# Transformer block in split fp16: output products of the last batch moved between the last score units and behind the last AV

## The chip, the cores and the metric

The kernel runs on one core of one Trainium2 chip. The metric is the device time of one execution, in microseconds (us). Three executions before the change took 1926.81, 1930.75 and 1939.71 us; the median is 1930.75 us.

## The reference

For x of 16 batches x 512 rows x 512 values, with xn the layer norm of x over its last axis, the reference computes

```
x + attention(xn) + ffn(xn)
attention: q, k, v = xn @ w_qkv.T + b_qkv; 16 heads of 32; softmax(causal(q k.T / sqrt(32))) v; then @ w_out.T + b_out
ffn:       (silu((xn @ gate.T) * gate_s) * ((xn @ up.T) * up_s)) @ down.T * down_s      (512 -> 1408 -> 512)
```

## The kernel before

**Number format.** Every fp32 operand is split into a high and a low fp16 half, and a product is the sum of three fp16 products (high x high, high x low, low x high). The gate, up and down weights are ternary, so for them two products do.

**Groups and units.** A batch has four groups of four heads, so there are 64 groups (0 to 63, `NGRP`). The scores of a group are worked off in ten units, `U = 10`, numbered n = 0 to 639 (`NU` = 640). I call those of the last group unit 0 to unit 9 (n = 630 to 639). A unit is one PSUM bank of score tiles (widths 512, or 384 + 128, or 256 + 256); four banks (0 to 3) are used in turn. Each unit passes through these steps:

- TensorE: `scores(n)`, 1 or 2 products (tile `stk`), which wait until the low half of unit n - 4 is done (`v_lo`), since the bank is used again.
- VectorE: `maximum(n)` (line 548; it appears as ISA or CUSTOM_DVE_ANT_0). ScalarE: `exponent(n)` (L466).
- VectorE: `reciprocals` once for two units (L539), ScalarE scales them (L454).
- ScalarE: `high(n)` (L458) writes the high half of the probabilities to `phl`; VectorE: `low(n)` (L558) the low half.
- SyncE: `turn_p` (L912) turns the finished tiles with a DMA transpose into `pt`. The queue issues them in program order. The last three transposes of a group wait for the low halves of unit 8 (two of them) and of unit 9 (the last one).
- TensorE: `av(G)`, 48 products of 32 columns of weights (tiles `pt`, `vv`), two score units into the next group; of the last group it stands at n = 644 (`NU + AV_K`). ScalarE drains it (L434), POOL splits it into `att` (L752 high, L754 low, semaphore `p_al`).

**The rest of a batch's end.** `down_product(b, t)` makes 128 rows (t = 0 to 3) of the down projection: 22 products of 512 columns. VectorE scales the result (`down_scale`, L592, into the buffer `q_0`) and POOL adds it to `res` (`down_add`, L781). The output projection of 128 rows is 12 products of 512 columns (`out_products`), three for each of the four groups of the batch. In the last batch nine of them per row block, those of the first three groups, are issued ahead of the last AV (36 in all), into banks 4, 5, 0 and 1 (`early_bank`), and the three of the last group behind it (12 in all). VectorE adds the result to `res` (`out_add`, L585), and SyncE stores it (L958).

**The flag.** The fast path holds only for inputs in range. VectorE gathers the tests in `check_end` (L613 to L628, 12 instructions), TensorE sums the flags over the partitions with one fp32 product (line 391), VectorE turns it into an integer in `check_flag` (L632 to L637). Behind the block all engines meet at a barrier (L963), load the flag (L52), and branch over the general path (L55).

**What sets the order.** All five engines run a program written out by hand in a loop over n; within a step n the calls stand in a fixed order. TensorE issues in program order, and so do the others: an instruction that waits holds up all behind it. `d_at`, `av_at` and, for the change, `early_at` say at which n a product stands.

Of the kernel before, what the change touches and what calls it, by code (L numbers as in the profile page):

```python
# [46 lines left out]
def fused_block(nc, x, w_qkv, b_qkv, w_out, b_out, gate, up, down, gate_s, up_s, down_s, out):  # L47
    B = x.shape[0]
    args = (B, x, w_qkv, b_qkv, w_out, b_out, gate, up, down, gate_s, up_s, down_s, out)
    with ExitStack() as ctx:  # L50
        flag = fast_path(nc, ctx, *args)
        general = nc.values_load(flag[0:1, 0:1], min_val=0, max_val=3)  # L52
    with nc.If(general > 0), ExitStack() as ctx:
        general_path(nc, ctx, *args)
    nc.end_ifs()  # L55
# [11 lines left out]
def fast_path(nc, ctx, B, x, w_qkv, b_qkv, w_out, b_out, gate, up, down, gate_s, up_s, down_s, out):  # L67
# [3 lines left out]
    NU = U * NGRP  # L71
    NF = 2 * NI * B
# [16 lines left out]
    bq, gsh, cis, half, ones = (carve(n) for n in (12, NI, NI, 1, 1))  # L89
# [4 lines left out]
    flag, flag_i = fl[0:1, 0:4], fl[0:1, 4:5].bitcast(I32)  # L94
    flag_p = lst[0]
# [36 lines left out]
    d_last = sem("d_last")  # L132
    d_y = [sem(f"d_y{i}") for i in range(4)]
# [15 lines left out]
    for b in range(B):  # L149
        if b == 0:  # L150
            v_at[0] = (0, 1, 0)
            v_at[1] = (0, 1, 1)
        else:
            v_at[40 * b] = (b, 0, 0)
            v_at[40 * b + 1] = (b, 0, 1)
            v_at[40 * b + 17] = (b, 1, 0)
            v_at[40 * b + 29] = (b, 1, 1)
        for t, k in enumerate((19, 21, 37, 39)):
            d_at[40 * b + k] = (b, t)
        if b < B - 1:  # L160
            for t, k in enumerate((47, 48, 49, 51)):
                o_at[40 * b + k] = (b, t)
# [27 lines left out]
            res_at[16 + t if b == 0 else 40 * b + (12, 13, 15, 17)[t]] = (b, t)  # L190
    LAST = NU + 6
    early_bank = [bank[i] for i in (4, 5, 0, 1)]

# [54 lines left out]
    def tensor_program(eng):  # L250
# [42 lines left out]
        def av(G):  # L293
            b, g = divmod(G, 4)
            for qt in range(3):
                w.wait_ge(d_pt[qt][0], 16 * (2 * G + 2))
            for p in range(2):
                w.wait_ge(d_pt[3][p], 16 * (G + 1))
            w.wait_ge(v_vl, 4 * b + 2 * (g // 2) + 2)
            bk = job_bank_free(("av", G))  # L300
            for kt in range(4):
                for k, (vp, pp) in enumerate(((0, 0), (1, 0), (0, 1))):
                    for j in range(4):
                        step = 12 + 2 * (j % 2) + pp
                        a = step * kt + 2 * (j % 2) + pp + kt
                        i = mm(bk[32 * j:32 * j + 32, 128 * kt:512], vv[:, vp, kt, 128 * g + 32 * j:128 * g + 32 * j + 32],
                               pt[j // 2][:, a:a + step * (3 - kt) + 1:step, :], kt == 0 and k == 0, kt == 3 and k == 2,
                               tile_position=(0, 32 * j))
            i.then_inc(s_av, 1)

        def out_products(bk, t, lo, hi):
            prods = [(kt, ap, wp) for kt in range(4) for ap, wp in ((0, 0), (0, 1), (1, 0))]
            for kt, ap, wp in prods[lo:hi]:
                i = mm(bk[:, :], att[:, ap, kt, 128 * t:128 * t + 128], wout[:, wp, kt], kt == 0 and not ap and not wp, kt == 3 and ap == 1)
            return i

        def o(b, t):
            for k in range(4):
                w.wait_ge(*ready["wout", k])
            w.wait_ge(p_al, 4 * b + 4)  # L320
            bk = job_bank_free(("o", b, t))
            out_products(bk, t, 0, 12).then_inc(s_o, 1)
# [39 lines left out]
        for n in range(LAST):  # L362
            if n < NU:
                scores(n)
            if NU <= n < NU + 4:
                t = n - NU
                w.wait_ge(p_al, 4 * B - 1)
                w.wait_ge(v_fh, NF // 2)
                w.wait_ge(v_fa, NF)
                if t >= 2:  # L370
                    w.wait_ge(v_lo, NU - 5 + t)
                out_products(early_bank[t], t, 0, 9).then_inc(s_oe, 1)
            if n in d_at:
                down_product(*d_at[n])
            if n in av_at:
                av(av_at[n])
            if n in qk_at:
                qk(*qk_at[n])
            if n in v_at:
                v(*v_at[n])  # L380
            if n in o_at:
                o(*o_at[n])
            for f in f_at.get(n, ()):
                gate_up(f)
        w.wait_ge(s_oe, 4)
        w.wait_ge(p_al, 4 * B)
        for t in range(4):
            out_products(early_bank[t], t, 9, 12).then_inc(s_o, 1)
        w.wait_ge(v_chk, 1)
        w.wait_ge(v_lo, NU)  # L390
        eng.matmul(bank[3][0:1, 0:3], ones[:, :], flag_p[:, 0:3], start=True, stop=True).then_inc(s_flag, 1)


    def scalar_program(eng):
# [114 lines left out]
    def vector_program(eng):  # L509
# [166 lines left out]
        for n in range(LAST):  # L676
            if n % 2 == 0 and 2 <= n <= NU:
                reciprocals(n - 2)
            if n < NU:
                maximum(n)  # L680
            if n - 1 in d_at:
                down_scale(*d_at[n - 1])
            for f in f_at.get(n - 1, ()):
                hidden(f)
            if 2 <= n <= NU + 1:
                low(n - 2)
            if n - 1 in v_at:
                v_low(*v_at[n - 1])
            if n - 1 in o_at:
                out_add(*o_at[n - 1])  # L690
            if n in norm_at:
                b, t = norm_at[n]
                w.wait_ge(d_xin[t % 2], 16 * xin_turn["norm", b, t])
                statistics(4 * b + t, t, xin[t % 2][:, :])
            if n - 4 in norm_at:
                b, t = norm_at[n - 4]
                hl = xhl[t % 2]
                w.wait_ge(p_xh, 4 * b + t - 3)
                w.wait_ge(v_xs, 4 * b + t + 1)
                eng.tensor_tensor(hl[:, 1], xin[t % 2][:, :], hl[:, 0], ALU.subtract).then_inc(v_xl, 1)  # L700
            if n - 2 in norm_at:
                b, t = norm_at[n - 2]
                scaled(4 * b + t, t, xin[t % 2][:, :])
            if n - 1 in wout_at:
                wout_low(wout_at[n - 1])
            if n in peak_at:
                check_peak(peak_at[n])
            if 0 <= n - 40 * (B - 1) < 19:
                check_most(n - 40 * (B - 1))
            if n == NU:  # L710
                check_end()
        for t in range(4):
            out_add(B - 1, t)
        check_flag()


    def gpsimd_program(eng):
# [165 lines left out]
    def sync_program(eng):  # L883
# [72 lines left out]
        for t in range(4):  # L956
            w.wait_ge(v_oy, 4 * (B - 1) + t + 1)
            eng.dma_start(out[B - 1, 128 * t:128 * t + 128, :], res[t][:, :]).then_inc(d_last, 16)  # L958
        for t in range(4):
            w.wait_ge(d_y[t], 16 * (B - 1))  # L960
        w.wait_ge(d_last, 64)

    with nc.Block() as block:  # L963
        block.tensor(tensor_program)
# [2 lines left out]
        block.gpsimd(gpsimd_program)  # L967
        block.sync(sync_program)

    return flag_i  # L970


def general_path(nc, ctx, B, x, w_qkv, b_qkv, w_out, b_out, gate, up, down, gate_s, up_s, down_s, out):
# [217 lines left out]
```

## Time and profile before

| | |
|---|---|
| median of three executions | 1930.75 us |
| the profiled execution, its own time | 1925.77 us |
| its span | 1922.4 us |
| granted TensorE clock, mean | 0.996 of full |
| PE busy | 1858.9 us (97%) |
| DVE busy | 1505.5 us (78%) |
| ACT busy | 1443.0 us (75%) |
| POOL busy | 1264.4 us (66%) |

The span is the time from the first to the last recorded instruction; the execution's own time is 3.4 us longer. PE is TensorE, DVE is VectorE, ACT is ScalarE, POOL is GpSimd, SPq is the queue of SyncE. A name such as L252 is the line of the kernel; all large products are issued from one helper, so they have the same line and are told apart by their tiles.

### The profile page before, as it was taken

To read this page: it belongs to the slowest core of one execution; us is meant where nothing else is said; L and a number is where in the kernel's file an instruction comes from. 1 tells how busy PE (TensorE), PEld (TensorE's weight loads), DVE (VectorE), ACT (ScalarE), POOL (GpSimd) and SP (SyncE) were. 2 spreads that over 40 slices of the span, in tenths; PEclk is the share of its full clock that TensorE was granted. 3 is DMA by queue.
4 is the path that set the end of the run, shared out by engine and by line. 5 is a ranking of instruction groups with operands and counts; after the bars stand their busy time and mean duration, and the time that the engine had idled before them with its cause. 6 is when DMAs were issued, how large, how long until landed. Compare 5 with 4: busy or idle time off the path is not lost.

```text
span 1922.4 us, 44220 instructions
## 1 busy us (share of the span) xinstructions
PE 1858.9 (97%) x14978; PEld 1220.4 (63%) x14978; DVE 1505.5 (78%) x4516; ACT 1443.0 (75%) x4263; POOL 1264.4 (66%) x1799
## 2 busy tenths in 40 slices
PE   6889999999999999999999999999999999999996
PEld 4556666666656666676666666666566666766663
DVE  4887778787787877778777787877878777787885
ACT  4786777868778787787867778687787877778684
POOL 5765857758576685766758576575666757576462
PEclk9999999999999999999999999999999999999998
DMA  9978969879797897979889798886978779687684
GB/s 227 160 158 159 186 130 194 149 159 181 132 197 144 171 168 136 196 132 190 152 155 187 133 192 134 161 159 134 189 128 169 150 140 183 131 182 138 121 163 94
DMA packets 818551, 305.93 MB, mean 159 GB/s; under 512 B 756176, under 2 KB 793168, under 8 KB 818320
## 3 DMA queue, kind: packets, MB, share of 16 engines
q1 hardware_dynamic: 796176, 240.79, 69.6%
q0 software_dynamic: 22144, 62.27, 13.0%
q8 instruction: 119, 1.95, 0.4%
q14 instruction: 112, 0.92, 0.1%
HBM read 55.59 MB, written 16.78 MB: 38 GB/s over the span
## 4 chain that ended last, share of the span: by engine, by line
PE 75%; DVE 11%; POOL 5%; ACT 5%; issue 2%; DMA 2%; SPq 1%; POOLq 0%; ACTq 0%; DVEq 0%
PE bank L252 75%; DVE phl L558 3%; ACT phl L458 2%; DVE bank L548 2%; DVE res L585 1%; ACT bank L466 1%; DVE xhl L700 1%; POOL ht L771 1%; DVE small L523 1%; DMA pt<-phl 1%; POOL qkp L744 1%; DVE fh L573 1%; DVE ft L568 1%; POOL att L754 0%; POOL ht L769 0%
## 5 line engine op out<-in xcount | busy, mean ns | idle before, releaser
L466 ACT ACTIVATE bank<-bank,small 128x512 f32<-128x512 f32 (+3 forms) x1024 | 516.8, 506 | 215.2 <-DVE small L548 214.6
L558 DVE SCALAR_TENSOR_TENSOR phl<-bank,small,phl 128x512 f16<-128x512 f32 (+3 forms) x1024 | 526.1, 545 | 139.3 <-ACT phl L458 136.2
L548 DVE CUSTOM_DVE_ANT_0 bank<-bank,mask 128x512 f32<-128x512 f32 (+3 forms) x1024 | 483.6, 503 | 179.9 <-PE bank L252 177.4
L458 ACT ACTIVATE phl<-bank,small 128x512 f16<-128x512 f32 (+3 forms) x1024 | 501.0, 532 | 29.6 <-DMA pt<-phl 19.0
L252 PE MATMUL bank<-xnT,wg 128*128 128x256 f16 x2816 | 365.7, 272 | 4.5 <-DVE fh L573 4.5
L252 PE MATMUL bank<-xnT,wu 128*128 128x256 f16 x2816 | 364.9, 273 | 0.0
L252 PE MATMUL bank<-xnT,wqkv 128*128 128x512 f16 x1536 | 353.4, 380 | 2.8 <-DMA xnT<-xhl 2.8
L252 PE MATMUL bank<-wd,ht 128*128 128x512 f16 x1408 | 314.5, 379 | 4.4 <-POOL ht L771 4.4
L252 PEld LDWEIGHTS bank<-xnT,wg 128*128 128x128 f16 x2816 | 263.0, 97 | 65.5 <-DVE fh L573 5.3
L252 PEld LDWEIGHTS bank<-xnT,wu 128*128 128x128 f16 x2816 | 275.6, 98 | 31.9
L252 PE MATMUL bank<-stk 96*128 96x512 f16 (+3 forms) x1024 | 244.8, 300 | 16.0 <-DVE phl L558 11.9
L771 POOL TENSOR_TENSOR ht<-fh,ht 128x256 f16<-128x256 f32 x352 | 237.4, 675 | 29.3
L252 PEld LDWEIGHTS bank<-xnT,wqkv 128*128 128x128 f16 x1536 | 148.1, 98 | 169.5 <-issue 4.7
L765 POOL TENSOR_TENSOR fh<-fh,ft 128x256 f32<-128x256 f32 x176 | 127.9, 727 | 185.1 <-DVE ft L568 184.8
L252 PEld LDWEIGHTS bank<-wd,ht 128*128 128x128 f16 x1408 | 136.0, 98 | 161.9 <-POOL ht L771 6.7
L769 POOL TENSOR_SCALAR ht<-fh 128x256 f16<-128x256 f32 x352 | 144.1, 410 | 126.3 <-DVE fh L573 109.5
L415 ACT ACTIVATE ft<-bank,small 128x256 f32<-128x256 f32 x352 | 170.4, 485 | 71.9 <-PE bank L252 71.4
L466 ACT ACTIVATION_READ_ACCUMULATOR bank<-bank,small 128x1 f32 x1024 | 215.7, 211 | 0.0
L252 PE MATMUL bank<-wqkv,xnT 128*128 128x256 f16 x1536 | 181.3, 275 | 14.4 <-DMA xnT<-xhl 14.4
L252 PE MATMUL bank<-wout,att 128*128 128x512 f16 x768 | 178.6, 383 | 3.5 <-POOL att L754 2.9
L252 PEld LDWEIGHTS bank<-wqkv,xnT 128*128 128x128 f16 x1536 | 150.9, 99 | 39.6 <-DVE wqkv L515 14.4
L781 POOL TENSOR_TENSOR res<-res,q 128x512 f32<-128x512 f32 x64 | 81.2, 1268 | 144.2 <-DVE q L592 143.8
(97 smaller groups left out, 2193.1 us busy)
## 6 DMA issues: line engine op xcount, KB each, us to landing
stk<-qkp SPq DMA_DIRECT2D x768, 64.0 KB, 2.2
res<-in_x_dram POOLq DMA_DIRECT2D x64, 256.0 KB, 4.7
xin<-in_x_dram POOLq DMA_DIRECT2D x60, 256.0 KB, 3.9
out_dram<-res POOLq DMA_DIRECT2D x60, 256.0 KB, 4.2
pt<-phl SPq DMA_TRANSPOSE x512, 4.3
xin<-in_gate_dram POOLq DMA_DIRECT2D x11, 256.0 KB, 3.9
xin<-in_up_dram POOLq DMA_DIRECT2D x11, 256.0 KB, 4.6
xin<-in_down_dram POOLq DMA_DIRECT2D x11, 256.0 KB, 3.6
```

What stands on the lines that cost most here:

```text
L252: mm = lambda o, lhs, rhs, start, stop, **k: eng.matmul(o, lhs, rhs, start=start, stop=stop, skip_group_check=True, **k)
L415: eng.activation(ft[f % 3][:, :], bank[4 + f % 2][:, 0:256], ACT.Tanh, scale=gsh[:, k:k + 1]).then_inc(a_ft, 1)
L458: i = eng.activation(part(qt, j)[:, j % 2, 0], pb[:, off:off + W], ACT.Copy, scale=st_r[:, c:c + 1])
L466: i = eng.activation(pb[:, off:off + W], pb[:, off:off + W], ACT.Exp, bias=st_m[:, c:c + 1], scale=-1.0, accum_out=st_s[:, c:c + 1])
L523: eng.bn_stats(st[:, 0:6], xi).then_inc(v_bn, 1)
L548: i = eng.tensor_tensor_reduce(out=bk[:, off:off + W], in0=bk[:, off:off + W], in1=mask[:, 512 - W:512], scale=-(32.0 ** -0.5) / (QS * QS) ...
L558: i = eng.scalar_tensor_tensor(part(qt, j)[:, j % 2, 1], pb[:, off:off + W], st_r[:, c:c + 1], part(qt, j)[:, j % 2, 0], ALU.mult, ALU.sub ...
L568: eng.scalar_tensor_tensor(tt[:, :], tt[:, :], 1.0, bk[:, 0:256], ALU.add, ALU.mult).then_inc(v_fa, 1)
L765: eng.tensor_tensor(hh[:, :], hh[:, :], ft[f % 3][:, :], ALU.mult).then_inc(p_fm, 1)
L769: eng.tensor_scalar(hs[:, 0], hh[:, :], 1.0, 1.0, op0=ALU.mult, op1=ALU.mult).then_inc(p_hh, 1)
L771: eng.tensor_tensor(hs[:, 1], hh[:, :], hs[:, 0], ALU.subtract).then_inc(p_fl, 1)
L781: eng.tensor_tensor(res[t][:, :], res[t][:, :], dtmp[:, :], ALU.add).then_inc(p_dy, 1)
```

## The change

Six things change, all in the last batch or behind it:

1. The output products of row blocks 0 and 1 for the first three groups (18) move from behind the last score unit to between the units: six behind unit 6, nine behind unit 7, three behind unit 8 (`early_at`). They wait for POOL's split of groups 61 and 62 (`p_al`) and for the last hidden tiles (`v_fh`, `v_fa`).
2. The down products of row blocks 2 and 3 (44 products) move from n = 637 and 639 to n = 640 and 641, so both stand behind unit 9.
3. The output products of row blocks 2 and 3 for the first three groups (18) move behind the last AV (`early_behind_av`).
4. VectorE's `check_end` moves from n = 640 to n = 642, behind the low half of unit 9, and the flag product moves ahead of the last 12 output products.
5. `check_flag` stands ahead of the four last `out_add` instead of behind them.
6. SyncE's waits for the stores leave the block and stand behind the load of the flag, in front of SyncE's branch.

```diff
--- before.py
+++ after.py
@@ -48,8 +48,9 @@
     B = x.shape[0]
     args = (B, x, w_qkv, b_qkv, w_out, b_out, gate, up, down, gate_s, up_s, down_s, out)
     with ExitStack() as ctx:
-        flag = fast_path(nc, ctx, *args)
+        flag, stored = fast_path(nc, ctx, *args)
         general = nc.values_load(flag[0:1, 0:1], min_val=0, max_val=3)
+        stored()
     with nc.If(general > 0), ExitStack() as ctx:
         general_path(nc, ctx, *args)
     nc.end_ifs()
@@ -155,7 +156,7 @@
             v_at[40 * b + 1] = (b, 0, 1)
             v_at[40 * b + 17] = (b, 1, 0)
             v_at[40 * b + 29] = (b, 1, 1)
-        for t, k in enumerate((19, 21, 37, 39)):
+        for t, k in enumerate((19, 21, 37, 39) if b < B - 1 else (19, 21, 40, 41)):
             d_at[40 * b + k] = (b, t)
         if b < B - 1:
             for t, k in enumerate((47, 48, 49, 51)):
@@ -190,6 +191,9 @@
             res_at[16 + t if b == 0 else 40 * b + (12, 13, 15, 17)[t]] = (b, t)
     LAST = NU + 6
     early_bank = [bank[i] for i in (4, 5, 0, 1)]
+
+    early_at = {NU - 4: ((0, 0, 6),), NU - 3: ((0, 6, 9), (1, 0, 6)), NU - 2: ((1, 6, 9),)}
+    early_behind_av = {NU + AV_K: (2, 3)}
 
 
 
@@ -314,6 +318,19 @@
                 i = mm(bk[:, :], att[:, ap, kt, 128 * t:128 * t + 128], wout[:, wp, kt], kt == 0 and not ap and not wp, kt == 3 and ap == 1)
             return i
 
+        def early_products(t, lo, hi):
+            w.wait_ge(p_al, 4 * B - 2)
+            if hi > 6:
+                w.wait_ge(p_al, 4 * B - 1)
+            if t < 2:
+                w.wait_ge(v_fh, NF // 2)
+                w.wait_ge(v_fa, NF)
+            else:
+                w.wait_ge(v_lo, NU - 5 + t)
+            i = out_products(early_bank[t], t, lo, hi)
+            if hi == 9:
+                i.then_inc(s_oe, 1)
+
         def o(b, t):
             for k in range(4):
                 w.wait_ge(*ready["wout", k])
@@ -362,18 +379,14 @@
         for n in range(LAST):
             if n < NU:
                 scores(n)
-            if NU <= n < NU + 4:
-                t = n - NU
-                w.wait_ge(p_al, 4 * B - 1)
-                w.wait_ge(v_fh, NF // 2)
-                w.wait_ge(v_fa, NF)
-                if t >= 2:
-                    w.wait_ge(v_lo, NU - 5 + t)
-                out_products(early_bank[t], t, 0, 9).then_inc(s_oe, 1)
+            for t, lo, hi in early_at.get(n, ()):
+                early_products(t, lo, hi)
             if n in d_at:
                 down_product(*d_at[n])
             if n in av_at:
                 av(av_at[n])
+            for t in early_behind_av.get(n, ()):
+                early_products(t, 0, 9)
             if n in qk_at:
                 qk(*qk_at[n])
             if n in v_at:
@@ -382,13 +395,13 @@
                 o(*o_at[n])
             for f in f_at.get(n, ()):
                 gate_up(f)
-        w.wait_ge(s_oe, 4)
-        w.wait_ge(p_al, 4 * B)
-        for t in range(4):
-            out_products(early_bank[t], t, 9, 12).then_inc(s_o, 1)
         w.wait_ge(v_chk, 1)
         w.wait_ge(v_lo, NU)
         eng.matmul(bank[3][0:1, 0:3], ones[:, :], flag_p[:, 0:3], start=True, stop=True).then_inc(s_flag, 1)
+        w.wait_ge(s_oe, 4)
+        w.wait_ge(p_al, 4 * B)
+        for t in range(4):
+            out_products(early_bank[t], t, 9, 12).then_inc(s_o, 1)
 
 
     def scalar_program(eng):
@@ -707,11 +720,11 @@
                 check_peak(peak_at[n])
             if 0 <= n - 40 * (B - 1) < 19:
                 check_most(n - 40 * (B - 1))
-            if n == NU:
+            if n == NU + 2:
                 check_end()
+        check_flag()
         for t in range(4):
             out_add(B - 1, t)
-        check_flag()
 
 
     def gpsimd_program(eng):
@@ -956,9 +969,6 @@
         for t in range(4):
             w.wait_ge(v_oy, 4 * (B - 1) + t + 1)
             eng.dma_start(out[B - 1, 128 * t:128 * t + 128, :], res[t][:, :]).then_inc(d_last, 16)
-        for t in range(4):
-            w.wait_ge(d_y[t], 16 * (B - 1))
-        w.wait_ge(d_last, 64)
 
     with nc.Block() as block:
         block.tensor(tensor_program)
@@ -967,7 +977,12 @@
         block.gpsimd(gpsimd_program)
         block.sync(sync_program)
 
-    return flag_i
+    def stored():
+        for t in range(4):
+            nc.sync.wait_ge(d_y[t], 16 * (B - 1))
+        nc.sync.wait_ge(d_last, 64)
+
+    return flag_i, stored
 
 
 def general_path(nc, ctx, B, x, w_qkv, b_qkv, w_out, b_out, gate, up, down, gate_s, up_s, down_s, out):
```

TensorE, from unit 5 of the last group up to the last AV; the tiles say which product it is (`stk` scores, `wd` down, `wout` output). Before:

```order
L252 MATMUL bank<-stk 128x512 x2
L252 MATMUL bank<-stk 128x384
L252 MATMUL bank<-stk 128x128
L252 MATMUL bank<-wd,ht 128x512 x22
L252 MATMUL bank<-stk 128x384
L252 MATMUL bank<-stk 128x128
L252 MATMUL bank<-stk 128x256 x2
L252 MATMUL bank<-wd,ht 128x512 x22
L252 MATMUL bank<-wout,att 128x512 x36
L252 MATMUL bank<-pt,vv 32x512 x12
```

With the change, the same place of TensorE:

```order
L256 MATMUL bank<-stk 128x512 x2
L256 MATMUL bank<-wout,att 128x512 x6
L256 MATMUL bank<-stk 128x384
L256 MATMUL bank<-stk 128x128
L256 MATMUL bank<-wout,att 128x512 x9
L256 MATMUL bank<-stk 128x384
L256 MATMUL bank<-stk 128x128
L256 MATMUL bank<-wout,att 128x512 x3
L256 MATMUL bank<-stk 128x256 x2
L256 MATMUL bank<-wd,ht 128x512 x44
L256 MATMUL bank<-pt,vv 32x512 x12
```

Nothing is added: 44 down products and 18 of the 36 output products stand ahead of the AV, in another order, and 22 fewer products of 512 columns stand between units 7 and 8, nine in their place.

TensorE behind the last AV, from its last 12 products on. Before:

```order
L252 MATMUL bank<-pt,vv 32x256 x12
L252 MATMUL bank<-pt,vv 32x128 x12
L252 MATMUL bank<-wout,att 128x512 x12
L391 MATMUL bank<-small 1x3
L963 UNCONDITIONAL_BRANCH
```

With the change, the same place of TensorE:

```order
L256 MATMUL bank<-pt,vv 32x256 x12
L256 MATMUL bank<-pt,vv 32x128 x12
L256 MATMUL bank<-wout,att 128x512 x18
L400 MATMUL bank<-small 1x3
L256 MATMUL bank<-wout,att 128x512 x12
```

Eighteen output products and the flag product now stand between the AV and the last 12 products.

VectorE, from behind the row maximum of unit 8 (`low` of unit 7 is the 128x384 and 128x128 pair ahead of the reciprocal, `low` of unit 8 the pair behind it). Before:

```order
L592 TENSOR_TENSOR q_0<-bank,dsc 128x512
L558 SCALAR_TENSOR_TENSOR phl_1<-bank,small,phl_1 128x512
L548 ISA bank,small<-bank,mask 128x256
L548 ISA small 128x1
L548 ISA bank,small<-bank,mask 128x256
L548 ISA small 128x1
L558 SCALAR_TENSOR_TENSOR phl<-bank,small,phl 128x384
L558 SCALAR_TENSOR_TENSOR phl<-bank,small,phl 128x128
L539 RECIPROCAL small<-small 128x4
L592 TENSOR_TENSOR q_0<-bank,dsc 128x512
L558 SCALAR_TENSOR_TENSOR phl<-bank,small,phl 128x384
L558 SCALAR_TENSOR_TENSOR phl<-bank,small,phl 128x128
```

With the change, the same place of VectorE:

```order
L571 SCALAR_TENSOR_TENSOR phl_1<-bank,small,phl_1 128x512
L561 ISA bank,small<-bank,mask 128x256
L561 ISA small 128x1
L561 ISA bank,small<-bank,mask 128x256
L561 ISA small 128x1
L571 SCALAR_TENSOR_TENSOR phl<-bank,small,phl 128x384
L571 SCALAR_TENSOR_TENSOR phl<-bank,small,phl 128x128
L552 RECIPROCAL small<-small 128x4
L571 SCALAR_TENSOR_TENSOR phl<-bank,small,phl 128x384
L571 SCALAR_TENSOR_TENSOR phl<-bank,small,phl 128x128
L605 TENSOR_TENSOR q_0<-bank,dsc 128x512
L571 SCALAR_TENSOR_TENSOR phl<-bank,small,phl 128x256 x2
```

The two `down_scale` instructions have left their places ahead of the low halves of units 6 and 8; the first now stands ahead of the low half of unit 9, the second behind it.

## Rows read from the trace of the kernel before

**Rows 1.** The chain of waits, end of the span; columns: start us, length us, what.

```profile
1904.60 1.84 PE bank L252 x48
...
1909.31 5.29 PE bank L252 x12
...
1914.70 0.69 DVE res L585
```

**Rows 2.** Timeline of TensorE (PE), from 1880 us; start us, us, instruction, count, idle before.

```profile
1886.25 0.39 PE L252 MATMUL bank<-stk 96*128 96x384 f16 x2 [1.83 <-DVE phl L558]
1886.48 4.91 PE L252 MATMUL bank<-wd,ht 128*128 128x512 f16 x22
1891.23 0.60 PE L252 MATMUL bank<-stk 96*128 96x384 f16 x4
...
1896.42 7.93 PE L252 MATMUL bank<-wout,att 128*128 128x512 f16 x36
...
1914.52 0.19 PE L391 MATMUL bank<-small 128*1 128x3 f32 x2
```

**Rows 3.** Timeline of VectorE (DVE), from 1886 us.

```profile
1890.22 0.18 DVE L539 RECIPROCAL small<-small 128x4 f32<-128x4 f32 x1 [0.48 <-ACT bank L466]
1891.65 0.57 DVE L548 CUSTOM_DVE_ANT_0 bank<-bank,mask 128x384 f32<-128x384 f32 x1 [1.25 <-PE bank L252]
...
1892.38 0.69 DVE L592 TENSOR_TENSOR q<-bank,dsc 128x512 f32<-128x512 f32 x1
...
1897.30 0.87 DVE L558 SCALAR_TENSOR_TENSOR phl<-bank,small,phl 128x384 f16<-128x384 f32 x2
...
1899.69 0.87 DVE L558 SCALAR_TENSOR_TENSOR phl<-bank,small,phl 128x256 f16<-128x256 f32 x2
```

**Rows 4.** Timeline of ScalarE (ACT), from 1886 us.

```profile
1896.04 1.57 ACT L458 ACTIVATE phl<-bank,small 128x384 f16<-128x384 f32 x4
```

**Rows 5.** Timeline of GpSimd (POOL), from 1886 us.

```profile
1885.59 1.16 POOL L754 TENSOR_TENSOR att<-q,att 128x512 f16<-128x512 f32 x1
```

**Rows 6.** The last attention transpose, read by its tile; issue time, then DMA to landing.

```profile
L912 SPq DMA_TRANSPOSE pt<-phl x1: 1307/1307/1307, 1901.3 to 1901.3; - x1
...
DMA to landing us min/median/max: 3.2/3.2/3.2
```

**Rows 7.** Timeline of SyncE's queue (SPq) from 1898 us: the first of the last three transposes.

```profile
1898.19 1.41 SPq L912 DMA_TRANSPOSE pt<-phl  x1
```

**Rows 8.** Timeline of PE: idle times near three us, early in the span.

```profile
63.40 1.05 PE L252 MATMUL bank<-xnT,wg 128*128 128x256 f16 x8 [2.87 <-DVE fh L573]
...
87.73 0.39 PE L252 MATMUL bank<-stk 96*128 96x384 f16 x2 [2.79 <-DVE phl L558]
...
107.02 4.04 PE L252 MATMUL bank<-xnT,wqkv 128*128 128x512 f16 x12 [2.79 <-DMA xnT<-xhl]
```

**Rows 9.** Stretches of PE: start:end us, length, busy (count), granted clock, DMA share, GB/s.

```profile
62.50:63.40 0.90, 0.01 (x1) 1.00 0.52 77
87.00:87.70 0.70, 0.00 (x0) 1.00 1.17 214
106.00:106.50 0.50, 0.00 (x0) 0.75 1.30 280
109.50:110.00 0.50, 0.50 (x3) 0.83 1.15 211
1908.50:1909.00 0.50, 0.00 (x0) 0.50 0.00 0
1915.00:1915.50 0.50, 0.00 (x0) 0.68 1.02 385
```

**Rows 10.** SyncE's waits after 1900 us, by line; durations ns, first and last start.

```profile
L43 SPq EVENT_SEMAPHORE  x2: 28/28/28, 1915.8 to 1917.5; - x2
```

**Rows 11.** The branch behind the flag, by line: PE's own.

```profile
L55 PEldq COMPARE_BRANCH  x1: 3783/3783/3783, 1918.6 to 1918.6; - x1
```

**Rows 12.** DMA queues from 1918.6 us to the end: packets, MB, share.

```profile
q14 instruction: 4, 0.03, 2.9%
```

More of the change, by code:

```diff
@@ L384, in tensor_program @@
                 gate_up(f)
+        w.wait_ge(v_chk, 1)
+        w.wait_ge(v_lo, NU)
+        eng.matmul(bank[3][0:1, 0:3], ones[:, :], flag_p[:, 0:3], start=True, stop=True).then_inc(s_flag, 1)
         w.wait_ge(s_oe, 4)
@@ L388, in tensor_program @@
             out_products(early_bank[t], t, 9, 12).then_inc(s_o, 1)
-        w.wait_ge(v_chk, 1)
-        w.wait_ge(v_lo, NU)
-        eng.matmul(bank[3][0:1, 0:3], ones[:, :], flag_p[:, 0:3], start=True, stop=True).then_inc(s_flag, 1)
     def scalar_program(eng):
```

## The prediction

> **What bounds the kernel now.** I read the page first: PE is busy for 97% of the span, but the change touches only the last 40 us, so shares of the whole say nothing of it. The views that count are the chain of waits at the end, the timelines of PE, VectorE and SyncE's queue from 1880 us on, and the rows behind the last store.
>
> The chain ends in three stages. The last AV starts at 1904.60; from its end, 1906.4, to 1909.31 PE stands while ScalarE drains and POOL splits it; then twelve output products take 5.29 us and the last add starts at 1914.70 [rows 1]. The reader should see two things in it. First, the twelve products cost 5.29 / 12 = 0.44 us each, while the 36 ahead of the AV cost 7.93 / 36 = 0.22 us each [rows 1, 2]: the granted clock is 0.50, the 1.2 GHz level, from 1908.5 on, after PE had been idle for 2 us, and is back only at about 1915.3 [rows 9]. Second, the AV looks as if it were held by PE (the output products end at about 1904.4), but the last transpose is issued at 1901.32 and lands 3.2 us later, at 1904.5 [rows 6]. So both end together, and taking products away ahead of the AV does not bring it forward by itself: the transposes must come earlier too.
>
> Behind the last add SyncE waits for the stores from 1915.8 to 1917.5 [rows 10]; then come the barrier, the load of the flag, and PE's branch of 3.78 us from 1918.6, which is the end of the span [rows 11].
>
> **The transposes: what the new order moves.** The chain to them runs over units 8 and 9. Before, unit 8's scores stood behind 22 down products (1886.48 to 1891.23), and VectorE waited 1.25 us for them before its maximum at 1891.65 [rows 2, 3].
>
> - Now nine output products stand there. They wait for POOL's split, which ends at 1885.59 + 1.16 = 1886.75 [rows 5]; with 9 x 0.22 = 1.98 us PE comes to unit 8 at about 1888.9. VectorE has the reciprocal at 1890.22 ahead of it, about 0.1 us long to the next start, so the maximum starts at about 1890.3: 1.3 us earlier. PE has one us of slack here, should POOL be late.
> - The down scale of 0.61 us (0.69 in its row, overlapped with the next) leaves the place between the maximum of unit 8 and the low half of unit 6 [rows 3]. From there VectorE is 1.3 + 0.6 = 1.95 us ahead.
> - ScalarE gains between 1.3 (unit 8) and 1.95 (unit 9); I take 1.6, since unit 7's high half stands between the two exponents. Its last four high halves then start at 1896.04 - 1.6 = 1894.4, and the two of unit 8 are done half of 1.57 us later [rows 4], at 1895.25. VectorE used to be in the second down scale then and started the low half of unit 8 at 1897.30 [rows 3]. Now it starts at 1895.3: 2.0 us earlier.
> - The low half of unit 9 is now behind a down scale that waits for the first 22 down products. They start behind unit 9, at about 1890.0, and end at 1890.0 + 22 x 0.22 = 1894.9, before VectorE gets there. If that cover were gone, it would be late by what the products are late.
> - SyncE issued the three last transposes in a row from 1898.19 to 1901.32 [rows 6, 7], so it is the low half of unit 8 that sets them. I move the landing by 2.0: 1902.5, the AV to 1902.6. Bounds: 1.3 (only the maximum's gain survives) and 2.5.
>
> PE is done with its 44 down products at 1890.0 + 9.7 = 1899.7. So it now idles for about 2.75 us **ahead of** the AV, where it was busy before.
>
> **From the AV to the last twelve products.** AV 1.84 us, then 18 output products, 3.97 us, then the flag product. The split of the AV takes 1909.31 - 1906.4 = 2.9 us and is covered by the 3.97. [...] AV start to first of the twelve: 1.84 + 3.97 + 0.5 = 6.3 us against 4.7 before: **+1.6**.
>
> **The last twelve.** With no idle time ahead of them they run at the full clock, 12 x 0.22 = 2.64 us in place of 5.29: **-2.65**. The adds (0.61 us each) keep pace with three products (0.66 us). `check_flag` costs nothing: it runs on VectorE before the first of the twelve is drained. `check_end`, 12 small instructions, runs after the second down scale at 1900, and has until 1908. The last `down_add` (1.3 us on POOL) ends near 1902, before the AV is drained.
>
> **The stores.** SyncE no longer waits ahead of the barrier: **-1.75** (1915.8 to 1917.5 and its wake-up). The last store, 2 us in flight, then ends about 3 us before PE's branch does, so the moved wait is covered.
>
> **The sum:** -2.0 + 1.6 - 2.65 - 1.75 = **-4.8 us** against the profiled execution's own 1925.77 us, so 1921.0. That execution is 5 us below the median shown, which moved in the same way gives 1926. Of the four executions known, two stand within 1.1 us of each other near 1926, and two above; I forecast **1924 us**, between the two readings.
>
> The Trainium skill ("TensorE: Matmul & The Clock Gate", Part 1) says that the default state of the array's clock is throttled and that activity releases it. By that the 30 products behind the AV run at the full clock and the sum stays -4.8, provided the AV's work counts as activity; the rows at 1909 to 1915 show a stretch of products in which it had not yet been released, by which the twelve would give nothing and the sum would be -2.1.
>
> **The rivals.**
>
> *The clock falls in the new idle time (0.35).* Early in this trace PE idled for 2.87 and 2.79 us and kept the full clock, and once for 2.79 us and lost it about 2 us into the idle time; it came back after 3.3 us or so [rows 8, 9]. The idle behind the last AV, 2.9 us, lost it for 6.7 us [rows 1, 9]. My 2.75 us is in the middle of these, so this is nearly as likely as the forecast. Of 3.3 to 6.7 us at half clock about 0.7 are idle; the other 2.7 to 6.0 us do half the work, a loss of 1.3 to 3.0 us. Sum -3.5 to -1.8: 1922.3 to 1924.0 by the profiled execution's count, 1927 to 1929 by the median's.
>
> *The same fall, and the clock stays low to the end (0.03): the one that ends slower.* Place: AV, 18 and 12 products. Price: each of them twice as long, 1.84 + 3.97 + 0 (the twelve were slow before too). Sum -2.0 + 1.6 + 5.8 - 1.75 = +3.7, 1929.4. It decides once more than 9.5 us of work is at half clock (half of it eats 4.8). For it: before, twelve products in a row, 5.3 us, did not bring the clock back until they were over. Against it: nowhere in the trace does low clock last beyond 6.7 us.
>
> *The transposes don't move (0.07).* They were held by the low half, but the transpose of units 6 and 7's tiles is now issued 2 us nearer to the ones before it, and transposes wait for one another. Then AV at 1904.6, PE idle for 4.7 us, and clock surely lost for 3 us or more: 0 + 1.6 - 2.65 - 1.75 + 2 = -0.8, 1925.0.
>
> *The branch gets slower (0.05).* PE's 3.78 us go with instruction packets, four in one queue [rows 11, 12]. Should a store still be in flight hold them up, at most the 1.75 us come back: -3.0, 1922.8. The Trainium skill ("Runtime: NRT & Kernel Launch", Instruction fetch mechanics) says that a taken branch outside the loaded part of the program must fetch its target by DMA; the packets agree. By my times the last store lands at 1914.5 and the fetch begins about then, so they hardly meet.
>
> *The 18 products between units delay the chain instead of filling it:* the first six fit into PE's 1.83 us of idle time ahead of unit 7 [rows 2] (6 x 0.22 = 1.3 us), the nine are counted above, and the three (0.66 us) end before unit 9's bank is free. I give this no chance of its own.
>
> **How the numbers follow.** Forecast 0.50, clock lost for a while 0.35, clock low to the end 0.03, transposes unmoved 0.07, branch 0.05. The cases lie between 1921 and 1929.4 by the profiled execution, and 5 us higher by the median; the shown executions themselves spread over 13 us. I take the range from 1918 (the sum by the profile with the transposes at their upper bound and the flag at its lower, 1920.2, and some scatter) to 1932 (the second case by the median, and scatter). A measurement of this kernel can tell about 1% (19 us) from no change; no case comes near it in either direction, and the few hundredths left are for scatter. Faster by over 1%: 0.01; within 1%: 0.98; slower by over 1%: 0.01.
>
> **What the profile after would show.** Right: VectorE's maximum of unit 8 no longer waits for PE; the last transpose issued near 1899.3; the AV near 1902.6; no idle time on PE from the AV to the end of the twelve products; these at 0.22 us each; no wait for the stores ahead of the barrier; span about 1917.6. The clock row between 1900 and 1910 decides between the first two cases. Wrong: an AV still at 1904.5, a row for the low half of unit 9 that waits for a down scale, or a branch on PE that starts 4.8 us earlier and ends at the same time as before.

## The result, and the profile after

The change took **1922.34 us** in the median of 20 executions (1919.03 to 1935.46), the kernel before 1929.69 us in as many (1921.13 to 1940.35). The ratio of the two is 0.997, 95% interval 0.9958 to 0.9983: 3.3 to 8.1 us less, well under 1%. The profiled execution of the change has a span of 1918.6 us and an own time of 1921.82 us; before it was 1922.4 and 1925.77.

Two executions of one kernel are not alike before the end begins. Unit 6's scores start at 1884.03 in the profile of before (the row ahead of those of [rows 2]), at 1885.24 in that of the change, and between 1880.8 and 1896.1 over all the traces read below. So I compare the **tail**: from the start of unit 6's score product (the last one of 512 columns) to the end of the span. The row of before is

```profile
1884.03 0.39 PE L252 MATMUL bank<-stk 96*128 96x512 f16 x1 [1.17 <-DVE phl L558]
```

and the tail is 1922.4 - 1884.03 = 38.4 us before and 1918.6 - 1885.24 = 33.4 us with the change, 5.0 less. PE's branch, which ends every span, took between 3.38 and 3.80 us in the traces below, without order, so a difference of tails under 0.4 us says nothing by itself.

TensorE (PE) of the change, timeline; start, length, instruction, count, idle time before it:

```profile
1885.24 0.39 PE L256 MATMUL bank<-stk 96*128 96x512 f16 x1 [1.15 <-DVE phl L571]
1885.46 1.46 PE L256 MATMUL bank<-wout,att 128*128 128x512 f16 x6
1887.46 0.39 PE L256 MATMUL bank<-stk 96*128 96x384 f16 x2 [0.54 <-DVE phl L571]
1888.00 2.12 PE L256 MATMUL bank<-wout,att 128*128 128x512 f16 x9 [0.15 <-POOL att L767]
1889.96 0.38 PE L256 MATMUL bank<-stk 96*128 96x384 f16 x2
...
1891.24 9.66 PE L256 MATMUL bank<-wd,ht 128*128 128x512 f16 x44
1903.85 1.81 PE L256 MATMUL bank<-pt,vv 128*32 128x512 f16 x48 [2.95 <-DMA pt<-phl]
1905.60 4.06 PE L256 MATMUL bank<-wout,att 128*128 128x512 f16 x18
1909.58 0.19 PE L400 MATMUL bank<-small 128*1 128x3 f32 x2
1909.71 2.76 PE L256 MATMUL bank<-wout,att 128*128 128x512 f16 x12
```

Against [rows 2]: the idle time ahead of unit 7 is 0.54 us, not 1.83; unit 8's scores are issued 4.7 us behind unit 6's, not 7.2; the AV starts 18.6 us behind them, not 20.6; and the twelve last products take 0.22 us each, not 0.44. The new idle time stands where it was forecast, ahead of the AV: 2.95 us, ended by a transpose.

VectorE (DVE), the rows that answer to [rows 3]:

```profile
1891.44 0.18 DVE L552 RECIPROCAL small<-small 128x4 f32<-128x4 f32 x1 [0.48 <-ACT bank L479]
1891.53 0.54 DVE L561 CUSTOM_DVE_ANT_0 bank<-bank,mask 128x384 f32<-128x384 f32 x1
...
1896.55 0.88 DVE L571 SCALAR_TENSOR_TENSOR phl<-bank,small,phl 128x384 f16<-128x384 f32 x2 [1.14 <-ACT phl L471]
1897.34 0.68 DVE L605 TENSOR_TENSOR q<-bank,dsc 128x512 f32<-128x512 f32 x1
1897.94 0.87 DVE L571 SCALAR_TENSOR_TENSOR phl<-bank,small,phl 128x256 f16<-128x256 f32 x2
...
1910.57 2.70 DVE L598 SCALAR_TENSOR_TENSOR res<-bank,res 128x512 f32<-128x512 f32 x4 [0.19 <-PE bank L256]
```

The maximum of unit 8 (1891.53) follows the reciprocal at once, where it had waited 1.25 us for PE. The low half of unit 8 starts 11.3 us behind unit 6's scores (13.3 before), and now waits for ScalarE's high half. The four last adds are one chain of 2.7 us, the pace of VectorE itself.

The chain of waits, against [rows 1]:

```profile
1898.91 1.61 SPq L925
...
1900.56 3.20 DMA pt<-phl
...
1912.58 0.69 DVE res L598
```

SyncE's issue of the second of the last three transposes and the flight of the last, 3.2 us, are now on the chain; with [rows 6] the flight is the same. ScalarE's and POOL's work on the last AV is off it.

Stretches of PE in its idle time ahead of the AV and in the twelve products (granted clock behind the count), to be held against [rows 9]:

```profile
1901.50:1902.50 1.00, 0.00 (x0) 1.00 0.72 137
1902.50:1903.80 1.30, 0.00 (x0) 1.00 0.53 96
...
1909.80:1912.40 2.60, 2.60 (x12) 1.00 0.09 35
```

The clock stays at 1.00 (2.4 GHz) through the idle time and to the end of the products. Last, PE's load of the flag and its branch (PEldq is a queue of PE; durations in ns, then the start):

```profile
L52 PEldq TENSOR_LOAD <-small x1: 762/762/762, 1914.1 to 1914.1; - x1
```

```profile
L56 PEldq COMPARE_BRANCH  x1: 3623/3623/3623, 1914.9 to 1914.9; - x1
```

The load takes 0.76 us and the branch 3.62 us; [rows 11] had 3.78 us. SyncE has no wait for the stores any more ahead of them.

### The profile page after: what moved, and what is told of

Same layout as the page of the kernel before. It is cut to its first block, busy times and chain, and to the rows that moved or that the text cites. A ratio compares the mean times of both kernels' runs of the same rounds, so it can differ in the third digit from the quotient of the medians.

```text
span 1918.6 us, 44219 instructions
## 1 busy us (share of the span) xinstructions
PE 1857.7 (97%) x14978; PEld 1220.3 (64%) x14978; DVE 1504.7 (78%) x4516; ACT 1441.9 (75%) x4263; POOL 1262.0 (66%) x1799
## 4 chain that ended last, share of the span: by engine, by line
PE 72%; DVE 11%; ACT 5%; POOL 5%; DMA 3%; issue 3%; SPq 1%; ACTq 0%; DVEq 0%; POOLq 0%
PE bank L256 72%; DVE phl L571 3%; ACT phl L471 3%; DVE bank L561 2%; DMA pt<-phl 2%; DVE res L598 1%; ACT bank L479 1%; DVE small L536 1%; POOL ht L784 1%; DVE xhl L713 1%; DVE fh L586 1%; POOL qkp L757 1%; DVE ft L581 1%; POOL ht L782 0%; POOL att L767 0%
```

## The experiments

The measure is the tail, in one trace per kernel unless said otherwise. Total times decide little here: the kernel before alone had medians of 1929.69, 1931.63 and 1927.31 us in three groups of executions. Two theories stand against each other all along: that the tail is set by the chain of transposes and by where PE's clock falls (mine), and that each part of the change has its own fixed price.

**stores_only.** The kernel before with part 6 alone.

```diff
     general = nc.values_load(flag[0:1, 0:1], min_val=0, max_val=3)
+    stored()
...
-        for t in range(4):
-            w.wait_ge(d_y[t], 16 * (B - 1))
-        w.wait_ge(d_last, 64)
```

> The kernel before with part 6 alone: SyncE waits for the last stores behind the load of the flag. Measure: the tail, from the first score product of unit 6 of the last group to the end of the span (before 38.4 us, the change 33.4 us). My theory (the wait for the stores was on the path and PE's branch now covers it): tail 36.6 to 36.8 us, 1.6 to 1.8 us less than before. Rival (the stores in flight hold up the load of the flag and the branch's instruction fetch, so the wait only moves): tail 38 us or more. Order of PE and VectorE as before; the twelve last products still at 0.44 us each.

Measured: tail 35.7 us, 1 us less than forecast. Ratio to before 0.9999 (0.9976 to 1.0023). From the start of the last add to the start of PE's branch it is 2.4 us, where before has 3.9: the wait was worth **1.5 us**. But the rest of the tail is not that of the first profile:

```profile
1895.46 6.15 PE L253 MATMUL bank<-wd,ht 128*128 128x512 f16 x22
...
1914.81 1.81 PE L253 MATMUL bank<-pt,vv 128*32 128x512 f16 x48 [0.24 <-issue]
1919.53 2.75 PE L253 MATMUL bank<-wout,att 128*128 128x512 f16 x12 [2.90 <-POOL att L755]
```

```profile
1895.40:1897.40 2.00, 2.00 (x7) 0.50 0.66 122
...
1919.60:1922.00 2.40, 2.40 (x12) 1.00 0.02 7
```

The second fence is of the granted clock. The clock fell ahead of unit 7's scores and the 22 down products behind them took 6.15 us in place of 4.91 [rows 2]; and it held through the 2.90 us behind the AV, so that the twelve took 2.75 us. My "still at 0.44 us each" was wrong. That put a new question: which falls belong to the kernel, and which to the single execution?

**stores_back.** The change with the waits for the stores inside the block again.

```diff
-        stored()
...
+        for t in range(4):
+            w.wait_ge(d_y[t], 16 * (B - 1))
+        w.wait_ge(d_last, 64)
```

> The change without part 6: SyncE waits for the stores inside the block, as before. My theory: tail 33.4 + 1.6 = 35.0 us, and the load of the flag again at 0.48 us instead of 0.76. Rival (the other parts cover nothing of it, or the store wait is worth nothing now): 33.4 us.

Measured: tail 34.8 us, ratio to before 0.998 (0.9957 to 1.0002). It is 1.4 us longer than with the change, and the load of the flag is back at its old length:

```profile
L52 PEldq TENSOR_LOAD <-small x1: 483/483/483, 1913.3 to 1913.3; - x1
```

From the start of the last add to PE's branch it is 4.0 us here and 2.4 in the change: the move is worth **1.6 us**. The load of the flag starts 3.4 us behind the start of the last add here and 1.5 us in the change, 1.9 less, and then takes 0.28 us longer (0.76 against 0.48 us), which goes with stores in flight.

**all_ahead.** The change with the 18 output products of part 3 ahead of the AV.

```diff
-    early_behind_av = {NU + AV_K: (2, 3)}
+    early_at[NU + 2] = ((2, 0, 9), (3, 0, 9))
+    early_behind_av = {}
```

> The change without part 3: the 18 output products of row blocks 2 and 3 stand ahead of the last AV, behind the down products. My theory: PE then reaches the AV about 1.1 us later than the last transpose lands (44 down products end at the same time, 3.97 us more follow), the 2.9 us of drain and split behind the AV are idle again, and the clock falls in them: twelve products at 0.44 us each, tail 33.4 + 1.1 - 1.1 + 2.65 = about 36.0 us. Rival (the clock was not the gain, it stays high or fell by chance): the twelve at 0.22 us, tail 33.4 us.

```profile
1903.34 4.05 PE L257 MATMUL bank<-wout,att 128*128 128x512 f16 x18
1907.32 1.81 PE L257 MATMUL bank<-pt,vv 128*32 128x512 f16 x48
...
1912.04 4.44 PE L257 MATMUL bank<-wout,att 128*128 128x512 f16 x12 [2.88 <-POOL att L768]
```

Measured: tail 34.55 us, ratio 0.9985 (0.9961 to 1.0009). The AV starts 19.5 us behind unit 6's scores, held by PE, and 2.88 us of idle time stand behind it again. The clock fell, but only when the twelve had begun (at 25.0 us in this measure; they start at 24.2), and they took 4.44 us, not 5.29. The direction is as expected, the size was too high by 1.4 us. With the clock left out, part 3 moves almost nothing: the twelve start 24.2 us behind unit 6's scores here and 24.5 in the change. What it changes is where the 2.9 us of idle time stand, and so which work a fall of the clock hits.

**units_as_before.** The change without parts 1 and 2.

```diff
-        for t, k in enumerate((19, 21, 37, 39) if b < B - 1 else (19, 21, 40, 41)):
+        for t, k in enumerate((19, 21, 37, 39)):
...
-    early_at = {NU - 4: ((0, 0, 6),), NU - 3: ((0, 6, 9), (1, 0, 6)), NU - 2: ((1, 6, 9),)}
+    early_at = {NU: ((0, 0, 9),), NU + 1: ((1, 0, 9),)}
```

> The change without parts 1 and 2: the 44 down products and the 18 output products of row blocks 0 and 1 stand between and behind the units as before; row blocks 2 and 3 stay behind the AV, and parts 4 to 6 stay. My theory (the transposes, not PE, set the AV): VectorE again waits for unit 8's scores, the last transpose is issued 2.0 us later than with the change, the AV starts 20.5 us behind unit 6's scores (18.6 with the change), PE idles for about 4 us ahead of it and the clock falls: tail 33.4 + 2.0 + 1.3 to 3.0 = 36.7 to 38.4 us. If the clock holds: 35.4. Rival (PE's own work held the AV, so it starts when PE is free): the AV at about 16.6 us, tail 31.5 us.

```profile
1892.67 6.60 PE L256 MATMUL bank<-wd,ht 128*128 128x512 f16 x22
...
1912.47 2.57 PE L256 MATMUL bank<-pt,vv 128*32 128x512 f16 x48 [4.13 <-DMA pt<-phl]
```

```profile
1908.40:1912.40 4.00, 0.00 (x0) 1.00 0.74 138
1912.50:1913.30 0.80, 0.80 (x18) 1.00 0.00 0
1913.50:1914.90 1.40, 1.40 (x32) 0.50 0.00 0
```

Measured: tail 38.5 us, ratio 0.9994 (0.9969 to 1.0019). PE was free long before and waited 4.13 us for the transposes, so the rival (PE holds the AV) falls. The AV starts at 22.2 us, 1.7 later than I said, because the clock fell at unit 7 here as well: 22 down products in 6.60 us. By the stretches of the granted clock in the second fence it held through the 4.13 us ahead of the AV and fell a second time about 0.9 us into the AV. In this trace, with the AV ahead of 18 products but the old order of the units, the whole gain is gone, the stores' part too; but two falls of the clock are in it, and without them I had forecast 35.4.

**nine_ahead and nine_again.** The change with row block 2's nine products ahead of the AV. Two traces of it.

```diff
-    early_behind_av = {NU + AV_K: (2, 3)}
+    early_at[NU + 2] = ((2, 0, 9),)
+    early_behind_av = {NU + AV_K: (3,)}
```

> The change, but row block 2's nine early output products stand ahead of the last AV (behind the down products) and only row block 3's nine behind it. My theory: with the change PE idles 2.95 us ahead of the AV for the transposes; nine products (2.0 us) fit in, so the AV still starts 18.6 us behind unit 6's scores. Behind it the nine others take 2.0 of the 2.9 us of drain and split, so the twelve start 4.7 us behind the AV's start in place of 5.86: tail 33.4 - 1.1 = 32.2 us. Both idle times are then about 1 us, so the clock should not fall in either. Rival (products ahead of the AV push it back, as the 18 did by 0.9 us): AV at 19.5, tail 33.2.

> The kernel nine_ahead, a second trace. My theory: AV at 18.5 us, twelve products at 23.3 us, tail 32.1 us, no fall of the clock between unit 6 and the last product, since no idle time is longer than 1.2 us. Rival (its first trace was luck): a fall in the tail, 33.4 us or more.

The timeline of PE in nine_ahead:

```profile
1906.81 2.11 PE L257 MATMUL bank<-wout,att 128*128 128x512 f16 x9
1909.86 1.81 PE L257 MATMUL bank<-pt,vv 128*32 128x512 f16 x48 [0.94 <-issue]
1911.61 2.12 PE L257 MATMUL bank<-wout,att 128*128 128x512 f16 x9
...
1914.58 2.75 PE L257 MATMUL bank<-wout,att 128*128 128x512 f16 x12 [0.73 <-POOL att L768]
```

Measured: tails of 32.1 and 32.4 us, ratio to before 0.997 (0.9951 to 0.9989), median 1920.73 us of 9 executions against 1927.31 for before. The AV starts 18.5 us behind unit 6's scores as in the change, the twelve 4.7 us behind that in place of 5.9, and no clock fell in either trace. By the trace it is the shortest tail of all; by total time it cannot be told from the change.

**check_end_back.** The change with VectorE's tests at their old place.

```diff
-            if n == NU + 2:
+            if n == NU:
```

> The change with VectorE's check_end at its old place, ahead of the low half of unit 9. My theory: nothing, tail 33.4 us. The 12 small instructions (1.7 us) delay the low half of unit 9 from 12.7 to about 14.4 us behind unit 6's scores, which ends at 15.3, just when SyncE is free for the last transpose (issued at 15.3). Rival (the low half of unit 9 sets the last transpose): AV 0.5 us or more later, tail 33.9 or more.

```profile
1902.20 3.16 PE L256 MATMUL bank<-pt,vv 128*32 128x512 f16 x48 [2.95 <-DMA pt<-phl]
```

Measured: tail 34.8 us. The AV starts at 18.6 us, as in the change, although VectorE's low half of unit 9 starts at 14.0: the place of `check_end` gives nothing. Nearly all of the extra 1.4 us is the AV's: 3.16 us for 1.81, since here the clock fell in the 2.95 us ahead of it.

**flag_last.** The change with the flag product and `check_flag` at the end.

```diff
-        w.wait_ge(v_chk, 1)
-        w.wait_ge(v_lo, NU)
-        eng.matmul(bank[3][0:1, 0:3], ones[:, :], flag_p[:, 0:3], start=True, stop=True).then_inc(s_flag, 1)
...
-        check_flag()
         for t in range(4):
             out_add(B - 1, t)
+        check_flag()
```

(The three lines of the product stand behind the twelve products instead.)

> The change with the flag product behind the twelve last output products and check_flag behind the last add, as before (parts 4's flag and 5 undone); the waits for the stores stay outside the block. My theory: the twelve start 0.13 us earlier, and VectorE ends 0.55 us later, where only SyncE's issue of the last store (0.4 us) covers it: tail 33.4 + 0.0 to 0.4 us. Rival (the flag's place is worth its 0.5 us or more): 33.9 or more.

Measured: tail 33.5 us, 0.1 more than with the change. The flag's place is worth nothing that this measure can show.

**six_between.** The kernel before with only six output products ahead of unit 7.

```diff
+            if n == NU - 4:
+                w.wait_ge(p_al, 4 * B - 2)
+                w.wait_ge(v_fh, NF // 2)
+                w.wait_ge(v_fa, NF)
+                out_products(early_bank[0], 0, 0, 6)
...
-                out_products(early_bank[t], t, 0, 9).then_inc(s_oe, 1)
+                out_products(early_bank[t], t, 0 if t else 6, 9).then_inc(s_oe, 1)
```

> The kernel before, with six of the nine early output products of row block 0 moved into PE's 1.8 us of idle time ahead of unit 7's scores; nothing else changes (stores, flag, down products as before). My theory (that idle time is what loses the clock in the 22 down products behind it, in three of four executions with the old order of units): these take 4.9 us, not 6.2 to 7.7, and the AV starts 1.3 us earlier on PE's side only, so it still stands at 20.5 us, held by the transposes, with about 1.2 us of idle time ahead of it; tail 38.4 us with a fall behind the AV, 35.7 without. Rival (something else in the old order, the down product itself, loses the clock): a fall within the 22 down products again, in about three of four executions.

```profile
1889.34 0.39 PE L252 MATMUL bank<-stk 96*128 96x384 f16 x2 [0.53 <-DVE phl L563]
1889.57 4.91 PE L252 MATMUL bank<-wd,ht 128*128 128x512 f16 x22
...
1907.65 1.81 PE L252 MATMUL bank<-pt,vv 128*32 128x512 f16 x48 [1.51 <-issue]
1912.37 2.75 PE L252 MATMUL bank<-wout,att 128*128 128x512 f16 x12 [2.90 <-POOL att L759]
```

Measured: tail 35.9 us, with no fall at all: the 22 down products take 4.91 us, and the twelve 2.75 us behind 2.90 us of idle time. The AV stays at 20.5 us though PE was free 1.5 us before it, as forecast. One trace does not prove that the six products hold the clock: with the gap open it held in one of five too. Against the rival (the down product loses the clock) speaks that in three of the four falls at this place the clock had fallen before the down product began, in stores_only at 1894.5 us, with the first down product at 1895.46.

**before_again, before_third and after_again.** The two kernels once more, for the clock.

> The kernel before, once more, for where the clock falls in the tail. My theory (the granted clock is a matter of the single execution: an idle time of 1.8 us ahead of unit 7 or of 2.9 us behind the AV may or may not lose it): a fall at one of these two places, tail 36 to 39 us. Rival (the clock always falls behind the last AV, as in the first profile): the twelve again at 0.44 us each and tail 38.4.

> The kernel before, a third trace. So far, in the tail, the clock fell ahead of or in unit 7's down product in three of four executions with the old order of units, and behind the AV in three of the four with 2.9 us of idle time there. My theory: at least one of the two falls shows here. Rival (the falls belong to certain kernels, not executions): the picture of the first trace, only the fall behind the AV.

> The change, a second trace, with 2.95 us of idle time ahead of the AV and none behind. My theory: AV at 18.6 us; tail 33.4 us if the clock holds (three of four executions so far), 34.8 if it falls there; no fall at unit 7. Rival (a fall at unit 7 also with the new order): 22 down products or the products between the units at half clock.

The timeline of PE in before_third, and the stretches ahead of the AV and in it in after_again:

```profile
1898.33 0.61 PE L252 MATMUL bank<-stk 96*128 96x384 f16 x2 [1.83 <-DVE phl L558]
1898.73 7.67 PE L252 MATMUL bank<-wd,ht 128*128 128x512 f16 x22
...
1924.30 4.44 PE L252 MATMUL bank<-wout,att 128*128 128x512 f16 x12 [2.90 <-POOL att L754]
```

```profile
1896.50:1898.00 1.50, 0.00 (x0) 1.00 0.60 116
1898.50:1899.30 0.80, 0.00 (x0) 0.60 0.22 42
1899.40:1901.50 2.10, 2.10 (x24) 0.50 0.00 0
```

Measured: tails of 40.1 and 40.3 us for before (38.4 in the first profile), 34.5 for the change (33.4). In both new traces of before the clock fell twice, ahead of or at unit 7's scores (22 down products in 7.7 us) and behind the AV, when the twelve had begun (4.44 us). The tails lie above the 36 to 39 us that I had expected of before_again, since both falls came. In the second trace of the change it fell once, ahead of the AV.

All fourteen traces, by the idle time in which, or within 1 us behind which, the clock fell:

| idle time of PE | kernels with it | fell |
|---|---|---|
| ahead of unit 7, 1.83 us | before (3 traces), stores_only, units_as_before | 4 of 5 |
| the same, filled to 0.54 us | the change (2), stores_back, all_ahead, check_end_back, flag_last, nine_ahead (2), six_between | 0 of 9 |
| behind the AV, 2.9 us | before (3), stores_only, all_ahead, six_between | 4 of 6 |
| ahead of the AV, 2.9 us | the change (2), stores_back, check_end_back, flag_last | 2 of 5 |
| ahead of the AV, 4.13 us | units_as_before | 1 of 1 |
| under 1.0 us on either side of the AV | nine_ahead (2) | 0 of 2 |

The 1.83 us do not stand alone: ahead of them PE does one score product, and ahead of that it is idle for 1.17 us more. The six products fill only the second of the two, so the table does not say whether 1.83 us alone would lose the clock.

## Why the prediction was right, and where it was not

The forecast was 1924 us, 4.8 us less than before by one trace; the executions say 3.3 to 8.1 less, the first pair of traces 5.0. The median of 1922.34 us is 1.7 below the forecast. By its steps:

- **The transposes, -2.0.** AV at 20.57 before, 18.61 after: -1.96. The maximum of unit 8 came at 6.3 us (forecast 1890.3 - 1884.0 = 6.3), the low half at 11.3 (11.3), the last transpose at 15.3 (15.3). units_as_before shows that PE alone would not have done it.
- **AV to the twelve, +1.6.** Measured 1909.71 - 1903.85 = 5.86 against 4.71, so +1.15. The 0.5 us that the sum has between the 18 products and the twelve is shown by no row and no run: the flag product costs 0.13, between 1909.58 and 1909.71, and starts before the modelled end of the fp16 product ahead of it, 1905.60 + 4.06 = 1909.66. The idle time ahead of the AV was 2.95 us; the prediction's own times give 1902.6 - 1899.7 = 2.9, not its 2.75.
- **The twelve, -2.65.** -2.5 between the first two traces. As a property of the kernels the term was mis-stated: I took the fall behind the AV as certain before. It came in 4 of 6 traces with that idle time, and then the twelve took 5.28 us once and 4.44 us three times, against 2.75. The other half of the step held: behind 18 products the twelve ran at the full clock in every trace, also where the clock had fallen ahead of the AV. Of the two readings that the prediction weighed, the traces agree with the one by which activity releases the clock (the Trainium skill, "TensorE: Matmul & The Clock Gate", Part 1): in the first trace of the change it never fell, but in after_again and check_end_back it fell ahead of the AV and was back at 1.00 before the 18 products began.
- **The stores, -1.75.** Measured -1.5 and -1.6. SyncE's wait does go, but the load of the flag takes 0.28 us longer with the stores in flight. The branch is not held up: 3.38 to 3.80 us over all the traces, 3.62 in the change.
- **The rivals.** The fall in the new idle time, which I gave 0.35, came in 2 of 5 traces and cost 1.1 and 1.4 us of tail (33.4 to 34.5 and 34.8), of which the AV has 1.3 in both: the low end of my 1.3 to 3.0. The clock never stayed low to the end. The transposes moved. The branch did not slow down.
- **What the prediction missed.** The idle time of 1.83 us ahead of unit 7 loses the clock too, in 4 of 5 traces with the old order, and the down products behind it then take 1.2 to 2.8 us more. The profile of before was the one in five in which it held, and I counted the filling of this gap as nothing. The six products moved there are part of the gain.

With the clock left out, the two kernels differ by 2.5 us: six_between, with the stores' wait as before and no fall, has a tail of 35.9, the change 33.4; 1.6 of the 2.5 are the stores, and 0.8 the AV (1.9 earlier) with what stands behind it (1.1 more). Averaged over the traces, three of before have 39.6 us and two of the change 33.9, a difference of 5.7, close to the 5.8 (1 - 0.997 of 1930) of the executions. By these five traces more than half of the gain is the clock, 3.2 of 5.7. With all fourteen pooled it is half: in the old order the fall at unit 7 delayed the AV by 1.8 us on average (5 traces) and the one behind the AV cost 1.3 (6 traces), in the new order the one ahead of the AV 0.5 (5 traces); that is 2.6 of 5.1. So few traces give no more than "about half". The sum was right in size because one fall taken as certain, 2.65 us, came near to these 2.6 us, what several uncertain ones cost on average. That was luck.

Not settled: what decides, at one and the same idle time, whether the clock falls. It wasn't tried to force it.

## What to carry to other kernels

Before the end of a kernel is re-ordered, find what lands last ahead of each stage: here a transpose that had been issued three in a row behind one low half, so moving products gave nothing until the score unit behind them came earlier. Products that are free to move are best used to fill idle times of TensorE of about 2 us and more, on both sides of a dependent product (nine ahead and nine behind had a shorter tail than 18 behind, though the total times do not tell them apart), since such an idle time costs its own length and, in a good part of the executions, the clock of the work behind it. One trace shows one draw of the clock; more traces of the kernel before would have shown the second gap.

## What the runs showed of the hardware

- The clock fell in or right behind an idle time of only 1.83 us (with 1.17 us of idle time and one product ahead of it) in four of five traces, and held through 2.9 us in others, once through 4.13 us until 0.9 us into the work behind; in before_third the work behind it ran slow for about 6 us.
- Where the clock fell late, the work paid only from there on: the same twelve products took 5.28 us where it fell ahead of them, 4.44 where it fell 0.5 to 0.9 us into them and 2.75 where it held, the AV 3.1, 2.57 and 1.81 us likewise.
- The load of the flag by all engines took about 0.5 us alone and about 0.8 us with stores of 256 KB in flight (PE's own 0.48 in five traces, 0.74 to 0.78 in nine). PE's branch behind it took 3.4 to 3.8 us either way, and ends the span in every trace.
